# A sandwich layer of banded attention and a feed-forward on eight cores: the halo rows in 16 partitions, the clears behind the layernorm of x, and two thirds of its last step by ScalarE

## The chip, the cores and the metric

The kernel runs on the 8 cores of one Trainium2 chip, in two dies of four. The metric is the device time of the slowest core in microseconds (us). Times inside a profile are counted from the start of that core's span. No data goes from one core to another.

## The reference

x has 8192 rows of 2048 (float32). With `ln` for a layernorm over the 2048 columns, the reference computes

```
x = x + ln(attn(ln(x)))       # attn: 32 heads of 64, each query sees keys i-8 .. i+7,
                              # scores scaled and weighted by distance, softmax, projection, bias
x = x + ln(ffn(ln(x)))        # ffn: 2048 -> 2048 with sign(W) * max|W|, gamma, beta
```

Each core owns 1024 rows and also needs 8 rows ahead of them and 8 behind them as keys and values: the halo.

## The kernel before

Every engine has its own instruction list, written out by hand, and takes it in order; semaphores tie the lists together. The stages are: (1) the front, which makes `lnT`, the layernorm of x, transposed and in bf16, and at the same time begins with (2) the 36 value tiles of 16 matmuls (L504); (3) 64 steps of attention with the query and key projections between them (L528); (4) the projection and the feed-forward in eight row tiles each (L591), with the rest of the layer.

**The front.** It has nine units. Unit 0 is the halo, 16 rows; units 1 to 8 are 128 rows each. One unit u passes through:

1. its load, `x_in[u]`: units 1 to 8 by the GpSimd queue (L399) in the order x1, first half of the value weights, x2, second half, x3 to x8, then the next block of value weights. `xbuf` has five places, so x6, x7 and x8 are issued only when units 1, 2 and 3 have been applied. The halo comes by SyncE's queue (L366, L367), into partitions 0 to 7 and 64 to 71 of a cleared buffer
2. `x_stats(u)` by VectorE: four BN statistics (L784) and their aggregate (L787)
3. `rstd` by ScalarE: Ln and Exp of the variance (L688, L689)
4. the last step of the layernorm by VectorE, (x - mean) * rstd to bf16 (L842), which raises `applied`
5. 16 transposes by TensorE in two halves (L487), each half into a PSUM bank of its own
6. `x_copy(u)`: VectorE copies the first half to `lnT` (L792) and raises `tx_v`; ScalarE copies the second (L660) and raises `tx_s`.

The lists run one unit ahead of their copies. VectorE's order for a unit is `x_stats(u)`, `x_copy(u-1)`, last step of u, and for u = 4, 6, 8 a copy of a value tile (`v_copy`). ScalarE's order is `rstd(u)`, `x_copy(u-1)`, and for u = 5, 7 a `v_copy`. TensorE's order is the transposes of units 0 and 1 and then, for each value tile n: its first 8 matmuls, the transposes of unit n + 2 (while there is one), its last 8 matmuls. The first half of tile n waits until both engines have copied unit n + 1:

```
t.wait_ge(tx_v, min(vt + 1, 8) + 1)
t.wait_ge(tx_s, min(vt + 1, 8) + 1)
```

and a transpose of unit u also waits until the copies of unit u - 1 have emptied its bank. After tile 6 there are no transposes left, and TensorE runs through value tiles alone.

**Clears.** Before unit 0, VectorE clears the halo's buffer (L826), `KTz`, `pstrip` and the last block of `VTOK` (L829 to L831), and makes `rolled`, a rotated identity (L833, L834). The halo's load waits for the first of these. `KTz`, `pstrip` and `rolled` are first used by attention, the cleared block of `VTOK` by value tile 8.

**SyncE's queue** loads the masks, the projection's bias and the first two feed-forward strips when all nine units are applied.

Of the kernel before, what the change touches and what calls it, by code (L numbers as in the profile page):

```python
# [15 lines left out]
D = 2048  # L16
# [18 lines left out]
LAG_T = LAG_S + 3  # L35
QUERIES = 2 * KWIN
LEAD = 3
FFN0 = 1 + NT - LEAD
# [19 lines left out]
def build_program():  # L58
# [15 lines left out]
    def sem(name):  # L74
        return nc.alloc_semaphore(name)
# [3 lines left out]
    at_small = base  # L79
    at_attn = at_small + 2592  # L80
    at_lnp = at_attn + 32 * OWN
# [7 lines left out]
    def place(name, cols, dtype, at, rows=128):  # L89
        return nc.alloc_sbuf_tensor_at(name, [rows, cols], dtype, offset=at)  # L90
# [14 lines left out]
    vwbf = place("vwbf", 2 * FULLW, BF16, at_attn)  # L105
    projb = place("projb", D, F32, at_lnp)
    fin = place("fin", 16, F32, at_small + 2528)
# [4 lines left out]
    xhalo = place("xhalo", D, F32, at_f + 56704)  # L112
    lnbf = place("lnbf", 2 * D, BF16, at_wp + 24576)
# [37 lines left out]
    ident_in_sem = sem("ident_in")  # L151
    halo_zero = sem("halo_zero")
    consts = sem("consts")
    var_ready = sem("x_var_ready")
    padded = sem("padded")
    x_in = [sem(f"x_in{u}") for u in range(9)]
    rstd_ready = sem("x_rstd_ready")
    applied = sem("x_applied")
    half_tx = sem("x_half_transposed")
# [7 lines left out]
    def xs(u):  # L167

        slot = (u - 1) % 5
        if u == 0:  # L170
            return xhalo[:]
        return xbuf[:, slot * D:(slot + 1) * D] if slot < 3 else (xbuf3 if slot == 3 else xbuf4)[:]

    def ls(u):
        return lnbf[:, u % 2 * D:(u % 2 + 1) * D]

    def mvc(u, i, n=1):
        return mv[:, 4 * u + i:4 * u + i + n]

    def x_evac(u, half):  # L180
        src = tpx[half].rearrange("p (k c) -> p k c", c=128)
        parts = [(0, 0, 8), (64, 8 + OWN, 8)] if u == 0 else [(0, 8 + 128 * (u - 1), 128)]
        return [(lnT3[:, half * 8:(half + 1) * 8, do:do + wd], src[:, :, so:so + wd]) for so, do, wd in parts]
# [176 lines left out]
    with nc.Block() as blk:  # L360

        @blk.sync
        def _(q):
            q.dma_start(out=ident[:], in_=ident_in).then_inc(ident_in_sem, 16)
            q.wait_ge(halo_zero, 1)
            q.dma_start(out=xhalo[0:8, :], in_=x_hbm[0:8, :]).then_inc(x_in[0], 16)  # L366
            q.dma_start(out=xhalo[64:72, :], in_=x_hbm[OWN + HALO:OWN + 2 * HALO, :]).then_inc(x_in[0], 16)  # L367
            q.wait_ge(applied, 9)
            q.dma_start(out=maskm[:], in_=masks[0]).then_inc(mask_in[0], 16)
# [25 lines left out]
        def _(g_):  # L395
            def load_x(u):
                if u >= 6:
                    g_.wait_ge(applied, u - 4)
                g_.dma_start(out=xs(u), in_=x_hbm[HALO + 128 * (u - 1):HALO + 128 * u, :]).then_inc(x_in[u], 16)  # L399
# [23 lines left out]
            load_v(1, 0, HALFW, FULLW)  # L423
            for u in range(3, 9):
                load_x(u)
# [53 lines left out]
        def _(t):  # L479
            def x_transposes(u):  # L480
                t.wait_ge(applied, u + 1)
                for half in range(2):
                    if u:
                        t.wait_ge(tx_v if half == 0 else tx_s, u)
                    for k8 in range(8):
                        kc = half * 8 + k8
                        last = t.transpose(tpx[half][:, k8 * 128:(k8 + 1) * 128],  # L487
                                           ls(u)[:, kc * 128:(kc + 1) * 128], ident[:])
                    last.then_inc(half_tx, 1)
# [114 lines left out]

            t.wait_ge(padded, 4)
            for G in range(STEPS + LAG_T):
# [49 lines left out]
        def _(s):  # L656
# [6 lines left out]
            def v_copy(n):  # L663
                if n == 17:
                    s.wait_ge(padded, 4)
# [25 lines left out]
            s.wait_ge(consts, 2)  # L691
# [84 lines left out]
        def _(v):  # L776
# [3 lines left out]
            def x_stats(u):  # L780

                v.wait_ge(x_in[u], 32 if u == 0 else 16)
                for c in range(4):
                    done = v_own.on(v.bn_stats(bnst[:, 24 * u + 6 * c:24 * u + 6 * c + 6],  # L784
                                               xs(u)[:, c * NB:(c + 1) * NB]))
                v.wait_ge(v_own.sem, done)
                v.bn_aggr(mvc(u, 0, 2), bnst[:, 24 * u:24 * u + 24]).then_inc(var_ready, 1)  # L787

# [6 lines left out]
            def v_copy(n):  # L795
                if n == 8:
                    v.wait_ge(padded, 4)
# [34 lines left out]
            v.wait_ge(ident_in_sem, 16)  # L832
            v.tensor_copy(rolled[:, 0:16], ident[:, 112:128])  # L833
            v.tensor_copy(rolled[:, 16:128], ident[:, 0:112]).then_inc(padded, 1)  # L834
            for u in range(9):
                x_stats(u)
                if u:
                    x_copy(u - 1)
                if u >= 2:
                    v.wait_ge(half_tx, 2 * (u - 2) + 2)  # L840
                v.wait_ge(rstd_ready, u + 1)
                v.tensor_scalar(ls(u), xs(u), mvc(u, 0), mvc(u, 2), ALU.subtract, ALU.mult).then_inc(applied, 1)  # L842
# [6 lines left out]
            v.wait_ge(padded, 4)  # L849
            v.wait_ge(mask_in[0], 16)  # L850
# [214 lines left out]
```

## Time and profile before

| what | before |
|---|---|
| median of 3 runs | 728.91 us (727.24 to 729.54) |
| the profiled execution's own time | 729.89 us |
| its span on the slowest core (core 3) | 728.4 us |
| spans of all cores | 720.7 to 728.4 us |
| TensorE busy | 659.3 us, 91% |
| VectorE busy | 425.7 us, 58% |
| ScalarE busy | 331.3 us, 45% |
| GpSimd busy | 205.5 us, 28% |
| data moved by DMA | 98.66 MB, mean 135 GB/s |

Between the span and the profiled time lie 1.49 us of start and end. In rows of instructions the first number is the start, the second the time from the first start to the last end of a merged group; in square brackets stands how long the engine had been idle and what ended that. PE is TensorE, PEld its weight loads, DVE VectorE, ACT ScalarE, POOL GpSimd, SPq SyncE's queue. In rows of DMA issues the last number is the time from issue to landing. Idle time of an engine that nothing waits for costs nothing.

### The profile page before, as it was taken

What the parts mean: (1) busy time and instruction counts of PE and PEld (TensorE: products, weight loads), DVE (VectorE), ACT (ScalarE), POOL (GpSimd) and SP (SyncE); (2) the same over time, 40 slices, a digit from 0 to 9 for tenths busy, and PEclk for the clock granted to TensorE, in tenths of its full rate; (3) what the DMA queues carried; (4) which work ended last, traced back from release to release, by engine and by line L of the source; (5) the groups of instructions that cost most, each with busy time, mean ns of one, the idle gap of its engine ahead of it and who ended that gap; (6) DMA issues with size and microseconds to landing.
All of it is one profiled execution on the core that took longest, in us unless ns stands there. A gap on an engine that the chain in (4) does not pass through costs nothing.

```text
span 728.4 us, 13295 instructions; the slowest of 8 cores (720.7 to 728.4 us)
## 1 busy us (share of the span) xinstructions
PE 659.3 (91%) x4048; PEld 356.1 (49%) x4048; DVE 425.7 (58%) x798; ACT 331.3 (45%) x888; POOL 205.5 (28%) x271
## 2 busy tenths in 40 slices
PE   0599999999999999999999999999989958689993
PEld 0354444445666666666666665444434424334441
DVE  7894110112667777777777776324776648777655
ACT  0222000001577777777777778402433404544244
POOL 2000010000666666666666667200001000000000
PEclk9999999999999999999999999999999989989997
DMA  8995949930447767667667765953434393744453
GB/s 187 278 233 142 177 71 154 169 53 1 59 62 118 125 119 122 121 117 123 117 117 119 120 112 91 162 154 61 143 115 139 104 334 117 231 146 144 145 199 118
DMA packets 18101, 98.66 MB, mean 135 GB/s; under 512 B 2274, under 2 KB 2274, under 8 KB 11490
## 3 DMA queue, kind: packets, MB, share of 16 engines
q0 software_dynamic: 10656, 67.11, 44.2%
q1 hardware_dynamic: 7378, 30.71, 17.2%
q8 instruction: 36, 0.59, 0.3%
q14 instruction: 31, 0.25, 0.1%
HBM read 114.59 MB, written 16.78 MB: 180 GB/s over the span
## 4 chain that ended last, share of the span: by engine, by line
PE 67%; DVE 11%; issue 10%; DMA 6%; ACT 3%; POOL 1%; DVEq 1%; ACTq 0%; POOLq 0%
PE bank L528 30%; PE bank L504 15%; PE bank L591 13%; DMA y_scratch<-abuf 6%; DVE bnst L784 3%; DVE abuf L921 3%; PE bank L544 2%; PE bank L552 2%; PE bank L553 2%; PE bank L565 2%; DVE abuf L961 1%; ACT tstrip L718 1%; ACT xnb L773 1%; DVE KTz L829 0%; DVE pstrip L830 0%
## 5 line engine op out<-in xcount | busy, mean ns | idle before, releaser
L528 PE MATMUL bank<-lnT,wbf 128*128 128x512 bf16 (+2 forms) x1280 | 248.4, 338 | 0.0
L528 PEld LDWEIGHTS bank<-lnT,wbf 128*128 128x128 bf16 x1280 | 122.8, 98 | 83.8 <-issue 0.4
L417 POOL TENSOR_TENSOR tstrip<-tstrip,maskb 128x288 f32<-128x288 f32 x128 | 93.5, 731 | 158.4 <-DVE tstrip L807 158.4
L504 PE MATMUL bank<-vwbf,lnT 128*128 128x512 bf16 (+1 forms) x576 | 128.8, 382 | 5.2 <-ACT lnT L660 5.2
L718 ACT ACTIVATE tstrip<-tstrip,soft 128x144 f32<-128x144 f32 x256 | 103.6, 405 | 44.4 <-DVE soft L866 44.0
L591 PE MATMUL bank<-Wp,attnT 128*128 128x512 bf16 x512 | 115.0, 383 | 0.5 <-DVE attnT L861 0.5
L591 PE MATMUL bank<-Wf,attnT 128*128 128x512 fp8e4 x512 | 113.7, 384 | 0.0
L807 DVE TENSOR_TENSOR tstrip<-bank,maskm 128x288 f32<-128x288 f32 x128 | 58.1, 454 | 64.1 <-PE bank L544 63.9
L504 PEld LDWEIGHTS bank<-vwbf,lnT 128*128 128x128 bf16 (+1 forms) x576 | 54.8, 97 | 75.4 <-issue 12.4
L591 PEld LDWEIGHTS bank<-Wf,attnT 128*128 128x128 bf16 x512 | 50.6, 99 | 61.2 <-issue 3.1
L591 PEld LDWEIGHTS bank<-Wp,attnT 128*128 128x128 bf16 x512 | 50.1, 99 | 59.3 <-issue 3.2
L453 POOL TENSOR_TENSOR pstrip<-tstrip,soft 128x576 bf16<-128x576 f32 x64 | 73.8, 1153 | 15.1 <-DVE soft L855 14.0
L800 DVE CAST VTOK<-bank 128x512 bf16<-128x512 f32 (+1 forms) x18 | 12.4, 689 | 89.1 <-PE bank L504 89.1
L668 ACT CAST VTOK<-bank 128x512 bf16<-128x512 f32 (+1 forms) x18 | 10.6, 586 | 92.9 <-PE bank L504 92.9
L708 ACT COPY ptbuf<-bank 128x576 bf16<-128x576 bf16 x64 | 41.0, 640 | 21.5 <-PE bank L553 20.8
L467 POOL DMA_DIRECT2D y_scratch<-abuf x8 | 4.4, 547 | 162.4 <-DVE abuf L961 162.4
L718 ACT ACTIVATION_READ_ACCUMULATOR tstrip<-tstrip,soft 128x1 f32 x256 | 48.1, 188 | 0.0
L866 DVE TENSOR_REDUCE soft<-tstrip 128x4 f32<-128x576 f32 x64 | 47.4, 740 | 0.0
L823 DVE TENSOR_REDUCE amaxc<-fwstage 128x1 f32<-128x1024 f32 x32 | 38.5, 1210 | 5.2 <-DMA fwstage<-ffn_wt 5.2
L683 ACT ACTIVATE Wf<-fwstage 128x1024 fp8e4<-128x1024 f32 x32 | 33.2, 1042 | 11.4 <-DMA fwstage<-ffn_wt 11.4
L552 PE MATMUL bank<-identb,pstrip 128*128 128x128 bf16 x256 | 35.3, 218 | 2.0 <-POOL pstrip L453 2.0
L544 PE MATMUL bank<-KTz,QT 128*128 128x288 bf16 x128 | 36.6, 286 | 0.0
(95 smaller groups left out, 696.3 us busy)
## 6 DMA issues: line engine op xcount, KB each, us to landing
fwstage<-ffn_wt SPq DMA_DIRECT2D x32, 512.0 KB, 6.6
wbf<-qk_strips POOLq DMA_DIRECT2D x32, 512.0 KB, 6.3
xbuf<-x_shard POOLq DMA_DIRECT2D x8, 1024.0 KB, 14.8
Wp<-proj_wt POOLq DMA_DIRECT2D x4, 2048.0 KB, 33.7
xre<-x_shard POOLq DMA_DIRECT2D x8, 1024.0 KB, 8.7
y_scratch<-abuf POOLq DMA_DIRECT2D x8, 1024.0 KB, 6.3
ybuf<-y_scratch SPq DMA_DIRECT2D x8, 1024.0 KB, 6.8
out<-fbuf POOLq DMA_DIRECT2D x7, 1024.0 KB, 8.6
```

The costliest lines, as they stand in the source:

```text
L417: g_.tensor_add(ts(g)[:, i * QUERIES:(i + 1) * QUERIES], ts(g)[:, i * QUERIES:(i + 1) * QUERIES], maskb[:, b * QUERIES:(b + 1) * QUERIES]) ...
L453: g_.tensor_mul(pu(r_)[:, :, 0:KWIN], ts3(r_), rtotal(r_)[:, :, None].broadcast_to([128, 4, KWIN])).then_inc(normed, 1)
L504: last = t.matmul(vbanks[n % 4][0:rows, :], lnT[:, kc * TOK + 128 * vt:kc * TOK + 128 * vt + rows], vwbf[:, (ng % 2) * FULLW + kc * NB:(ng ...
L528: last = t.matmul(qkbanks[gg % 3][:, 0:wd], wslot(2 * ph + is_k)[:, kc * 128:(kc + 1) * 128], lnT[:, kc * TOK + c0:kc * TOK + c0 + wd], st ...
L544: t.matmul(sbanks[i][:, 0:QUERIES], qt(ph)[:, 128 * b:128 * b + 128], ktz(ph)[:, :, 128 * b:128 * b + KWIN], start=True, stop=True).then_i ...
L552: t.transpose(tbank[:, u * 256:u * 256 + 128], pu(g)[:, u, 0:128], ident[:])
L591: last = t.matmul(bank(i), attnT[:, kc * OWN + 128 * t_:kc * OWN + 128 * t_ + 128], rhs, start=(kc == 0), stop=(kc == 15))
L708: s.copy(pt(h), tbank.rearrange("p (u c) -> p u c", c=256)[:, :, 0:KWIN]).then_inc(p_ev, 1)
L718: last = s.activation(ts3(m)[:, u, :], ts3(m)[:, u, :], AF.Exp, bias=neg_max(m)[:, u:u + 1], accum_out=total(m)[:, u:u + 1])
L807: v.tensor_mul(ts(g)[:, i * QUERIES:(i + 1) * QUERIES], sbanks[i][:, 0:QUERIES], maskm[:, b * QUERIES:(b + 1) * QUERIES]).then_inc(masked, 1)
L823: v.reduce_max(amaxc[:, i:i + 1], fw_slot(i), axis=AX.X, apply_absolute_value=True).then_inc(amaxed, 1)
L866: v.reduce_max(neg_max(m), ts3(m), axis=AX.X, negate=True).then_inc(maxed, 1)
```

## The change

Five things change, all in the front.

- **Halo.** The 16 halo rows lie in partitions 0 to 15 of `xhalo`, which has 16 partitions and isn't cleared. Their two loads are the first in SyncE's queue, ahead of the identity. All steps of unit 0 work on 16 partitions (`x_rows(0)`), and the transposes give 16 columns.
- **Clears.** `KTz` is cleared by VectorE after its last `x_copy(8)`, and `rolled` and `pstrip` after `v_copy(6)`. The block of `VTOK` is cleared by GpSimd between the issues of x5 and x6, with a semaphore of its own, `v_padded`.
- **Last step.** For the units 0, 2, 3, 5, 6 and 8 (`ACT_APPLIES`) ScalarE does the last step. VectorE negates the mean (one more instruction with 1 element per partition), ScalarE makes rstd, then -mean * rstd, then one Identity activation of 2048 elements with scale and bias. Units 1, 4 and 7 stay as they were.
- **Semaphores.** `applied` becomes `applied_v` and `applied_s`; `x_applied(u)` gives the one and its count for unit u. Who waited for `applied` now waits for the unit that matters.
- **A first Exp.** ScalarE runs an Exp of one element (`warm`) ahead of its loop.

```
@@ sync
-            q.wait_ge(halo_zero, 1)
+            q.dma_start(out=xhalo[0:8, :], in_=x_hbm[0:8, :]).then_inc(x_in[0], 16)
+            q.dma_start(out=xhalo[8:16, :], in_=x_hbm[OWN + HALO:OWN + 2 * HALO, :]).then_inc(x_in[0], 16)
             q.dma_start(out=ident[:], in_=ident_in).then_inc(ident_in_sem, 16)
-            q.wait_ge(applied, 9)
+            q.wait_ge(*x_applied(7))
+            q.wait_ge(*x_applied(8))
@@ gpsimd
-                    g_.wait_ge(applied, u - 4)
+                    g_.wait_ge(*x_applied(u - 5))
...
+            g_.memset(VTOK4[:, :, 8, :], 0.0).then_inc(v_padded, 1)
@@ scalar
+            def x_apply(u):
+                rows = x_rows(u)
+                s.wait_ge(s_own.sem, s_own.on(s.activation(mvc(u, 2)[0:rows], mvc(u, 1)[0:rows], AF.Ln,
+                                                          bias=epsv[0:rows, :])))
+                s.wait_ge(s_own.sem, s_own.on(s.activation(mvc(u, 2)[0:rows], mvc(u, 2)[0:rows], AF.Exp, scale=-0.5)))
+                s.wait_ge(s_own.sem, s_own.on(s.activation(mvc(u, 3)[0:rows], mvc(u, 0)[0:rows], AF.Identity,
+                                                          scale=mvc(u, 2)[0:rows])))
+                if u >= 2:
+                    s.wait_ge(half_tx, 2 * (u - 2) + 2)
+                s.activation(ls(u)[0:rows, :], xs(u), AF.Identity, scale=mvc(u, 2)[0:rows],
+                             bias=mvc(u, 3)[0:rows]).then_inc(applied_s, 1)
+            s.wait_ge(consts, 3)
+            s.activation(warm[:], warm[:], AF.Exp)
             for u in range(9):
-                rstd(mvc(u, 2), mvc(u, 1), u + 1, var_ready, epsv).then_inc(rstd_ready, 1)
+                if u in ACT_APPLIES:
+                    s.wait_ge(var_ready, u + 1)
+                    x_apply(u)
+                else:
+                    rstd(mvc(u, 2), mvc(u, 1), u + 1, var_ready, epsv).then_inc(rstd_ready, 1)
                 if u:
                     x_copy(u - 1)
@@ vector, x_stats
+                then(v.bn_aggr(mvc(u, 0, 2)[0:rows], bnst[0:rows, 24 * u:24 * u + 24]))
+                v.tensor_scalar(mvc(u, 0)[0:rows], mvc(u, 0)[0:rows], -1.0, None, ALU.mult).then_inc(var_ready, 1)
@@ vector, main list
-            v.memset(xs(0), 0.0).then_inc(halo_zero, 1)
-            v.memset(KTz[:], 0.0).then_inc(padded, 1)
-            v.memset(pstrip[:], 0.0).then_inc(padded, 1)
-            v.memset(VTOK4[:, :, 8, :], 0.0).then_inc(padded, 1)
...
             x_copy(8)
-            for n in range(6, 36, 2):
+            v.memset(KTz[:], 0.0).then_inc(padded, 1)
+            v_copy(6)
...
+            v.memset(pstrip[:], 0.0).then_inc(padded, 1)
+            for n in range(8, 36, 2):
                 v_copy(n)
```

## Rows read from the trace of the kernel before

**Rows 1.** The chain that ended last: its longest piece (start us, us, what).

```profile
64.20 102.58 PE bank L504 x472
```

**Rows 2.** Timeline of the start: clears, statistics of unit 0, table load.

```profile
4.16 3.52 DVE L829 MEMSET KTz<- 128x4160 bf16 x1 [0.81 <-issue]
12.33 1.76 DVE L831 MEMSET VTOK<- 128x2048 bf16 x1 [0.38 <-issue]
14.12 2.47 DVE L784 BATCH_NORM_STATS2 bnst<-xhalo 128x6 f32<-128x512 f32 x4
17.03 1.28 ACT L688 ACT_TABLE_LOAD   x1 [17.03 <-DVE mv L787]
```

**Rows 3.** DMA issues of x2, and of x3: KB, us from issue to landing.

```profile
xbuf<-x_shard POOLq DMA_DIRECT2D x1, 1024.0 KB, 16.8
...
xbuf<-x_shard POOLq DMA_DIRECT2D x1, 1024.0 KB, 25.9
```

**Rows 4.** Timeline of the GpSimd queue: issues of x2, and of x3 to x5.

```profile
2.79 0.54 POOL L399 DMA_DIRECT2D xbuf<-x_shard  x1
...
3.82 1.60 POOL L399 DMA_DIRECT2D xbuf<-x_shard  x3
```

**Rows 5.** A stretch of 3 us: busy times, granted clock, share of the DMA engines, GB/s.

```profile
27.00:30.00 3.00, 0.64 (x5) 0.26 (x4) 2.65 (x5) 1.40 (x3) 0.00 (x0) 1.00 1.02 322
```

**Rows 6.** Timeline of tile 0 and of units 2 and 3, with their neighbours.

```profile
29.75 3.57 PE L504 MATMUL bank<-vwbf,lnT 128*128 128x512 bf16 x8 [2.36 <-ACT lnT L660]
30.07 2.47 DVE L784 BATCH_NORM_STATS2 bnst<-xbuf 128x6 f32<-128x512 f32 x4
...
34.14 0.69 DVE L792 COPY lnT<-bank 128x1024 bf16<-128x1024 bf16 x1 [1.24 <-PE bank L487]
...
34.75 1.34 DVE L842 TENSOR_SCALAR lnbf<-xbuf,mv 128x2048 bf16<-128x2048 f32 x1
36.00 2.46 DVE L784 BATCH_NORM_STATS2 bnst<-xbuf 128x6 f32<-128x512 f32 x4
```

**Rows 7.** Timeline of a later unit: statistics, rstd, copy, half a tile, transposes.

```profile
41.48 2.47 DVE L784 BATCH_NORM_STATS2 bnst<-xbuf 128x6 f32<-128x512 f32 x4
...
42.28 1.06 PE L487 MATMUL bank<-identb,lnbf 128*128 128x128 bf16 x16
...
44.41 0.30 ACT L688 ACTIVATE mv<-mv,epsv 128x1 f32<-128x1 f32 x1 [3.99 <-DVE mv L787]
44.80 0.20 ACT L689 ACTIVATE mv<-mv 128x1 f32<-128x1 f32 x1
44.91 0.99 ACT L660 COPY lnT<-bank 128x1024 bf16<-128x1024 bf16 x1
...
46.05 1.89 PE L504 MATMUL bank<-vwbf,lnT 128*128 128x512 bf16 x8 [0.98 <-ACT lnT L660]
...
47.77 1.06 PE L487 MATMUL bank<-identb,lnbf 128*128 128x128 bf16 x16
```

**Rows 8.** Timeline: the last unit's transposes and copy, and a later tile's copy.

```profile
63.14 1.06 PE L487 MATMUL bank<-identb,lnbf 128*128 128x128 bf16 x16
63.86 0.69 DVE L792 COPY lnT<-bank 128x1024 bf16<-128x1024 bf16 x1 [1.54 <-PE bank L487]
...
80.05 0.69 DVE L800 CAST VTOK<-bank 128x512 bf16<-128x512 f32 x1 [6.33 <-PE bank L504]
```

**Rows 9.** Groups of ScalarE's instructions by shape: count, busy us, mean ns, idle.

```profile
L773 ACT ACTIVATE xnb<-abuf 128x2048 bf16<-128x2048 f32 x8 | 15.3, 1912 | 14.0 <-DVE abuf L961 14.0
...
L750 ACT ACTIVATE fbuf<-fbuf,tst 128x2048 f32<-128x2048 f32 x7 | 14.7, 2097 | 7.8 <-DVE tst L966 7.8
```

**Rows 10.** Timeline of TensorE behind two idle times of the last stage.

```profile
541.27 1.05 PE L651 MATMUL bank<-identb,xnb 128*128 128x128 bf16 x16 [3.39 <-DVE xnb L925]
...
656.76 1.05 PE L651 MATMUL bank<-identb,xnb 128*128 128x128 bf16 x16 [3.20 <-DVE xnb L925]
```

**Rows 11.** The stretch behind the first of them, columns as in rows 5.

```profile
542.20:545.60 3.40, 3.40 (x12) 1.27 (x10) 3.20 (x6) 1.42 (x4) 0.00 (x0) 0.52 0.00 0
```

More of the change, by code:

```diff
@@ L36 @@
 QUERIES = 2 * KWIN
+ACT_APPLIES = (0, 2, 3, 5, 6, 8)
 LEAD = 3
@@ L79, in build_program @@
     at_small = base
-    at_attn = at_small + 2592
+    at_attn = at_small + 2624
     at_lnp = at_attn + 32 * OWN
@@ L111, in build_program @@
     xbuf4 = place("xbuf4", D, F32, at_f + 41088)
-    xhalo = place("xhalo", D, F32, at_f + 56704)
+    xhalo = place("xhalo", D, F32, at_f + 56704, rows=2 * HALO)
     lnbf = place("lnbf", 2 * D, BF16, at_wp + 24576)
@@ L155, in build_program @@
     padded = sem("padded")
+    v_padded = sem("v_padded")
     x_in = [sem(f"x_in{u}") for u in range(9)]
     rstd_ready = sem("x_rstd_ready")
-    applied = sem("x_applied")
+    applied_v = sem("x_applied_v")
+    applied_s = sem("x_applied_s")
     half_tx = sem("x_half_transposed")
@@ L172, in xs, with x_rows, x_applied @@
         return xbuf[:, slot * D:(slot + 1) * D] if slot < 3 else (xbuf3 if slot == 3 else xbuf4)[:]
+    def x_rows(u):
+        return 2 * HALO if u == 0 else 128
+    def x_applied(u):
+        count = len([i for i in range(u + 1) if (i in ACT_APPLIES) == (u in ACT_APPLIES)])
+        return (applied_s if u in ACT_APPLIES else applied_v), count
     def ls(u):
@@ L423, in _ @@
             load_v(1, 0, HALFW, FULLW)
-            for u in range(3, 9):
+            for u in range(3, 6):
+                load_x(u)
+            g_.memset(VTOK4[:, :, 8, :], 0.0).then_inc(v_padded, 1)
+            for u in range(6, 9):
                 load_x(u)
@@ L480, in x_transposes @@
             def x_transposes(u):
-                t.wait_ge(applied, u + 1)
+                t.wait_ge(*x_applied(u))
+                rows = x_rows(u)
                 for half in range(2):
@@ L486, in x_transposes @@
                         kc = half * 8 + k8
-                        last = t.transpose(tpx[half][:, k8 * 128:(k8 + 1) * 128],
-                                           ls(u)[:, kc * 128:(kc + 1) * 128], ident[:])
+                        last = t.transpose(tpx[half][:, k8 * 128:k8 * 128 + rows],
+                                           ls(u)[0:rows, kc * 128:(kc + 1) * 128], ident[0:rows, 0:rows])
                     last.then_inc(half_tx, 1)
@@ L603, in _ @@
                 v_tile(n, 8, 16)
-            t.wait_ge(padded, 4)
+            t.wait_ge(padded, 3)
             for G in range(STEPS + LAG_T):
@@ L780, in x_stats @@
             def x_stats(u):
+                rows = x_rows(u)
                 v.wait_ge(x_in[u], 32 if u == 0 else 16)
                 for c in range(4):
-                    done = v_own.on(v.bn_stats(bnst[:, 24 * u + 6 * c:24 * u + 6 * c + 6],
+                    done = v_own.on(v.bn_stats(bnst[0:rows, 24 * u + 6 * c:24 * u + 6 * c + 6],
                                                xs(u)[:, c * NB:(c + 1) * NB]))
                 v.wait_ge(v_own.sem, done)
-                v.bn_aggr(mvc(u, 0, 2), bnst[:, 24 * u:24 * u + 24]).then_inc(var_ready, 1)
+                if u not in ACT_APPLIES:
+                    v.bn_aggr(mvc(u, 0, 2)[0:rows], bnst[0:rows, 24 * u:24 * u + 24]).then_inc(var_ready, 1)
+                    return
+                then(v.bn_aggr(mvc(u, 0, 2)[0:rows], bnst[0:rows, 24 * u:24 * u + 24]))
+                v.tensor_scalar(mvc(u, 0)[0:rows], mvc(u, 0)[0:rows], -1.0, None, ALU.mult).then_inc(var_ready, 1)
             def x_copy(u):
@@ L796, in v_copy @@
                 if n == 8:
[L797 removed]
+                    v.wait_ge(v_padded, 1)
                 v.wait_ge(tile_mm, n + 1)
@@ L824, in amax @@
                              apply_absolute_value=True).then_inc(amaxed, 1)
-            v.memset(xs(0), 0.0).then_inc(halo_zero, 1)
             v.memset(epsv[:], EPS).then_inc(consts, 1)
             v.memset(eps2[:], EPS * EPS).then_inc(consts, 1)
-            v.memset(KTz[:], 0.0).then_inc(padded, 1)
-            v.memset(pstrip[:], 0.0).then_inc(padded, 1)
-            v.memset(VTOK4[:, :, 8, :], 0.0).then_inc(padded, 1)
-            v.wait_ge(ident_in_sem, 16)
-            v.tensor_copy(rolled[:, 0:16], ident[:, 112:128])
-            v.tensor_copy(rolled[:, 16:128], ident[:, 0:112]).then_inc(padded, 1)
+            v.memset(warm[:], 0.0).then_inc(consts, 1)
             for u in range(9):
@@ L838, in _ @@
                     x_copy(u - 1)
[L839 to L842, printed above, removed]
+                if u not in ACT_APPLIES:
+                    if u >= 2:
+                        v.wait_ge(half_tx, 2 * (u - 2) + 2)
+                    v.wait_ge(rstd_ready, len([i for i in range(u + 1) if i not in ACT_APPLIES]))
+                    v.tensor_scalar(ls(u), xs(u), mvc(u, 0), mvc(u, 2), ALU.subtract, ALU.mult).then_inc(applied_v, 1)
                 if u in (4, 6, 8):
@@ L845, in _ @@
             x_copy(8)
-            for n in range(6, 36, 2):
+            v.memset(KTz[:], 0.0).then_inc(padded, 1)
+            v_copy(6)
+            v.wait_ge(ident_in_sem, 16)
+            v.tensor_copy(rolled[:, 0:16], ident[:, 112:128])
+            v.tensor_copy(rolled[:, 16:128], ident[:, 0:112]).then_inc(padded, 1)
+            v.memset(pstrip[:], 0.0).then_inc(padded, 1)
+            for n in range(8, 36, 2):
                 v_copy(n)
-            v.wait_ge(padded, 4)
+            v.wait_ge(padded, 3)
             v.wait_ge(mask_in[0], 16)
```

10 lines of the change are left out of this document (4 added, 6 removed).

## The prediction

> **What bounds the kernel now.** I read the chain that ended last first, then the timeline of the first 66 us, then DMA issues with landings, then ScalarE's groups and TensorE's idle times. TensorE sets the end: the longest piece of the chain is 472 value matmuls without a gap from 64.20 us on [rows 1]. They begin right behind the transposes of unit 8, which start at 63.14 [rows 8]. Behind this point TensorE's list is the same before and after the change, and everything later is tied to it. So the whole question is when the transposes of unit 8 start. A microsecond there is a microsecond of the end.
>
> What sets those 63.14 us? The clears keep VectorE until unit 0 starts at 14.12 [rows 2]. From there it has no gap worth the name: statistics, copy and last step follow each other at about 5.2 us a unit (30.07, 36.00, 41.48 [rows 6, 7]). But a second thing has nearly caught up. The load of x3 is issued at 3.82 and lands 25.9 us later, at 29.7 [rows 3, 4]; VectorE takes it up at 30.07 [rows 6]. The DMA engines are full in that stretch, share 1.02 [rows 5], and x3 stands behind x1, x2 and two blocks of value weights in one queue. A start of the statistics 9 us earlier therefore meets data that isn't there.
>
> **The steps and their prices.** I lay out the chain of the new lists, with each link from the nearest row.
>
> - Statistics to the start of ScalarE's last step, 4.15 us: statistics to Ln 2.93 (41.48 to 44.41); 0.25 for the negation of one element and its wait, an estimate after ScalarE's one-element instruction, 0.20 plus a wait of 0.09 (rounded down, as VectorE's are shorter); then Ln to a dependent instruction 0.39 (44.41 to 44.80), and Exp and the new one-element Identity 0.29 each (0.20 and the same wait of 0.09), together 0.97 [rows 7].
> - The last step on ScalarE, 1.95 us until its next instruction. Rows for 2048 elements give 1.91 with bf16 out and 2.10 with float32 out, scale and bias [rows 9]. I take 1.95, bounds 1.86 and 2.05, since the next instruction starts a little before the end. VectorE needs 1.25 for the same (34.75 to 36.00 [rows 6]).
> - ScalarE's copy to the matmuls that wait for it 1.15 (44.91 to 46.05); eight matmuls to the transposes behind them 1.72 (46.05 to 47.77) [rows 7], at the low clock 3.4 (tile 0's row of 3.57 with its end, against 1.89 [rows 6, 7]); transposes to VectorE's copy 0.7 (63.14 to 63.86 [rows 8]); this copy to VectorE's next instruction 0.6 (34.14 to 34.75 [rows 6]).
> - A `v_copy` on VectorE, 0.65, a little under its row of 0.69 [rows 8].
>
> **What goes off the path.** The halo's clear, the three others and `rolled` leave the front. They cost nothing later: VectorE idles 6.33 us between two copies of value tiles [rows 8], and `KTz` with 3.52 us [rows 2] and `pstrip`, nearly as large, each fit into such a gap; the bank of tile 6 is wanted again only four tiles later. Without that cover 7 us would be on the path. GpSimd's clear of `VTOK` takes between VectorE's 1.76 us [rows 2] and, as an estimate, twice that; behind it stands the issue of x6, which waits until unit 1 is applied, about 14.5 by the sum below, while the five loads are issued by 5.4 [rows 4]. Hidden, and x6 stands behind others in a full queue anyway. The halo's loads come first and are small; even landing at 12 they'd be ready before x2. SyncE's masks follow unit 8 as before. The 1.28 us of table load [rows 2] moves into idle time; a second one, if the first Exp loaded a table without Ln, would still lie ahead of x2.
>
> Two things of ScalarE decide the sum. One is whether a copy whose data is ready can pass an instruction that still waits. It can't in the trace: the transposes of unit 4 are over at 43.34, and ScalarE's copy of them starts at 44.91, right behind the Ln and Exp of unit 5, which had waited for VectorE until 44.41 [rows 7]. The Trainium skill says the same (TensorE: Matmul & The Clock Gate, Architectural detail): ScalarE and VectorE take their instructions strictly in order. By that rule the sum below stands at 66.9; if a copy could pass, the same links would give 62.7, and the change would cost nothing.
>
> The other is the price of 2048 elements. The rows give 1.91 and 2.10 [rows 9]. The skill's page on ScalarE (ScalarE: Activation LUTs, Step-by-step) has one element in 0.83 ns whatever the function, an estimate of 1.71 us here; the sum would be 0.9 lower by it. The rows are longer, and I go by them.
>
> **The sum.** The important thing is the order. ScalarE does the last step of unit u ahead of its copy of unit u - 1. The first half of value tile u - 2 waits for this copy, the transposes of unit u stand behind that half tile in TensorE's list, and VectorE's copy of unit u waits for these. Before, only a short rstd stood ahead of the copy. Now a statistics-to-copy delay of 6.1 us (4.15 + 1.95) does, and VectorE, in order, waits in turn. Tile 0's first half begins at 26.85 (x2 lands at 2.79 + 16.8 = 19.6 [rows 3, 4]; + 4.15 + 1.95 + 1.15). Cold matmuls and 16 transposes later its second half ends at about 33 us, and TensorE idles for 4 us. Then, at full clock:
>
> 1. x3 lands 29.7; ScalarE applies unit 3 at 33.85, copies unit 2 at 35.80; tile 1 at 36.95; transposes of unit 3 at 38.68; VectorE's copy 39.37; its last step of unit 4 at 39.97
> 2. + 1.25 + 0.65 of `v_copy`: statistics of unit 5 at 41.9. Before they began at 41.48 [rows 7]. The whole head start is gone here
> 3. unit 5: apply 46.0, copy of unit 4 at 48.0, tile 3 at 49.1, transposes 50.9, VectorE's copy 51.55, then `v_copy`: statistics of unit 7 at 52.8
> 4. unit 6 meanwhile: ScalarE, held by unit 5, a copy and a `v_copy`, applies it at 50.55, copies unit 5 at 52.5; tile 4 at 53.65; transposes 55.4; VectorE's copy 56.1, last step of unit 7 at 56.7; statistics of unit 8 at 57.95
> 5. unit 8: apply 62.1, copy of unit 7 at 64.05, tile 6 at 65.2, its transposes at 66.9.
>
> That is 66.9 against 63.14: 3.8 us later. The same links put through the old order give 62.9 for the old kernel, so the arithmetic is good to some 0.3 us. The data of units 4 to 8 isn't what holds it: each is wanted no more than 3 us earlier than it was, and never waited for, and unit 4's last step waits until 40 for TensorE.
>
> One term more, the clock. TensorE's idle time of 3.39 us in the last stage was followed by a stretch of 3.40 us with a granted clock of 0.52, the 1.2 GHz level [rows 10, 11], worth 1.7 us; behind 3.20 us of idle it stayed at 2.4 GHz [rows 10]. The new list has idle times of about 4.0 us (ahead of tile 1), 3.5 (tile 3) and 2.8 (tile 6). At the first a loss is likely, and tile 1 lies on the chain, so + 1.7: transposes of unit 8 at 68.6, 5.5 us later. A second such stretch at tile 3 gives 70.1, 7.0 later.
>
> The profiled 729.89 is its span of 728.4 and 1.49 around it; with 5.5 more it becomes 735.4. It stands 0.98 above the median, so I predict 728.91 + 5.5 = 734.4 us.
>
> **The rivals.** A measurement here tells about 0.3%, 2.2 us, from no change.
>
> - *Chain as above, one low-clock stretch at tile 1*: 734.4, chance 0.37. Its own range, with ScalarE's step between its bounds (two or three times 0.1 us) and landings 1 us earlier: 733.2 to 735.2.
> - *Clock never falls*: 728.91 + 3.8 = 732.7, chance 0.25. For it: 3.20 us of idle left the clock up. Against: 3.39 didn't.
> - *Clock falls twice or more*: 735.9, up to 738 with a third at tile 6, chance 0.18.
> - *Not slower: x3 lands earlier.* Place: the first link. If the halo's bytes out of the way and different crowding on the shared memory bring x3 down by 2 us or more, to 27.7, and the clock holds, the transposes of unit 8 start by 64.9, + 1.8: 730.7, inside 0.3%. Beyond 2 us VectorE's own pace takes over; with all data at hand the chain still gives 61.5, a gain of 1.6, 727.3. For it: DMA times vary. Against: the engines are full [rows 5] with the same bytes in the same order. Chance 0.14.
> - *Faster by over 0.3%*: needs unit 8's transposes by 60.9, under what the chain gives with all data at hand; a link would have to be much cheaper than its row. Chance 0.06.
> - *The removed clears don't count at all*, that is, nothing but DMA decides: the chain of links 2 to 5 would then not lengthen, and the time be the old one. It falls with link 2 above, and is part of the 0.14.
>
> **The numbers.** Slower 0.80, same 0.14, faster 0.06. The range reaches from the rival with earlier data, 730.5, to between the second and third loss of clock, 737.5; below it lies some 0.08, above it some 0.05.
>
> **What the new profile would show.** Statistics of unit 0 at about 5, of unit 3 at 29.7 with a wait for the DMA of `xbuf`; a gap of TensorE of about 4 us ahead of tile 1; VectorE's copies (L792's successor) waiting for TensorE in units 3, 5 and 6, where they never waited for long; ScalarE's copy behind each 1.9 us activation; transposes of unit 8 at 67 to 70. I'm wrong if they start before 63; most likely by data that came earlier, or by an order of copies other than I read.

## The result, and the profile after

The change makes the kernel slower: 736.1 us (median of 5 runs) against 728.91, a ratio of 1.0083 with a 95% interval of 1.0046 to 1.0120. Forecast were 734.4 us, in a range of 730.5 to 737.5. Some executions of a kernel here fall into a slower state of the chip, such as one of these five at 786.13 us; the ratios and their intervals leave them out, the medians given here don't, and the four others lie at 731.97 to 737.53 us with a median of 734.8. The same kernel timed a second time, on another occasion, gave 1.0043 (0.9998 to 1.0087). That interval reaches 1.0, so by the times alone the loss is small and its size is open. In that second comparison, as in the experiments 1 to 4, the kernel before was itself spread over 727 to 738 us; for that reason the steps below are judged by marks inside the traces and the times are given beside them. The profiled execution was the fastest of the five, 731.97 us, its slowest core being core 2 with a span of 730.4 us.

The timeline of core 2 in the changed kernel, cut to the chain that the prediction laid out (start us, us, what; in brackets the idle time ahead and what ended it):

```profile
4.66 2.46 DVE L817 BATCH_NORM_STATS2 bnst<-xhalo 16x6 f32<-16x512 f32 x4 [3.40 <-DMA xhalo<-x_shard]
...
28.56 2.47 DVE L817 BATCH_NORM_STATS2 bnst<-xbuf 128x6 f32<-128x512 f32 x4 [5.58 <-DMA xbuf<-x_shard]
...
30.03 1.06 PE L502 MATMUL bank<-identb,lnbf 128*128 128x128 bf16 x16
...
31.75 0.29 ACT L708 ACTIVATE mv<-mv,epsv 128x1 f32<-128x1 f32 x1 [5.20 <-DVE mv L824]
...
32.87 2.09 ACT L715 ACTIVATE lnbf<-xbuf,mv 128x2048 bf16<-128x2048 f32 x1
34.87 0.99 ACT L675 COPY lnT<-bank 128x1024 bf16<-128x1024 bf16 x1
...
36.01 2.82 PE L519 MATMUL bank<-vwbf,lnT 128*128 128x512 bf16 x8 [3.20 <-ACT lnT L675]
...
38.62 1.82 PE L502 MATMUL bank<-identb,lnbf 128*128 128x128 bf16 x16
...
39.79 0.69 DVE L829 COPY lnT<-bank 128x1024 bf16<-128x1024 bf16 x1 [4.34 <-PE bank L502]
...
42.25 2.46 DVE L817 BATCH_NORM_STATS2 bnst<-xbuf 128x6 f32<-128x512 f32 x4
...
49.69 2.85 PE L519 MATMUL bank<-vwbf,lnT 128*128 128x512 bf16 x8 [3.17 <-ACT lnT L675]
...
54.71 2.46 DVE L817 BATCH_NORM_STATS2 bnst<-xbuf 128x6 f32<-128x512 f32 x4
...
60.00 2.46 DVE L817 BATCH_NORM_STATS2 bnst<-xbuf 128x6 f32<-128x512 f32 x4
...
67.55 3.55 PE L519 MATMUL bank<-vwbf,lnT 128*128 128x512 bf16 x8 [3.00 <-ACT lnT L675]
...
70.92 1.07 PE L502 MATMUL bank<-identb,lnbf 128*128 128x128 bf16 x16
```

Read it from the top. The halo is there at 4.66, where VectorE used to be clearing until 14.12 [rows 2]. But VectorE then waits for data three times, the last for 5.58 us, and takes up x3 at 28.56, only 1.5 us before the old 30.07 [rows 6]. The transposes of unit 2 start at 30.03 and are over at 31.1, so their copy could start then. But ScalarE's list has the last step of unit 3 first, which runs from 32.87, and only behind it, at 34.87, comes the copy of unit 2, on which tile 1 waits until 36.01. The transposes of unit 3 stand behind this half tile, VectorE's copy waits 4.34 us for them, and the statistics of unit 5 begin at 42.25, later than the 41.48 of before [rows 7]. The same pattern returns at tile 3 and at tile 6. The transposes of unit 8 start at 70.92, in [rows 8] at 63.14.

The chain that ended last, between 25 and 72 us, goes through the same instructions (start us, us, what). What it calls "issue" at 32.91 is the last step on ScalarE: the chain has given it no name, but L715 fills just that time above.

```profile
3.83 24.64 DMA xbuf<-x_shard
28.56 2.48 DVE bnst L817 x4
...
32.91 1.96 issue
34.87 1.00 ACT lnT L675
35.87 0.14 issue
36.01 2.82 PE bank L519 x8
38.83 0.87 PE bank L502 x8
```

The waits of TensorE from 15 to 170 us (us in total, times, longest) say the same in one line; of the four, one is the start of tile 0, and the others stand ahead of tiles 1, 3 and 6.

```profile
PE bank L519 <- ACT lnT L675: 19.5, 4, 10.2
```

Behind each of these three idle times core 2 lost the clock, as the granted clock of three stretches shows (the column behind POOL; 1.00 is the 2.4 GHz level and 0.50 the 1.2 GHz level, and values between them are stretches with both; the others as in rows 5):

```profile
36.00:40.00 4.00, 3.99 (x21) 2.37 (x22) 0.21 (x1) 0.26 (x2) 0.58 (x2) 0.60 0.97 326
49.69:53.10 3.41, 3.41 (x16) 1.75 (x17) 0.00 (x0) 3.08 (x5) 0.00 (x0) 0.61 0.96 166
67.50:71.00 3.50, 3.45 (x10) 1.28 (x11) 0.00 (x0) 0.00 (x0) 0.00 (x0) 0.51 0.60 186
```

Core 6 of the same execution had idle times of 1.34, 3.49 and 3.00 us ahead of the same tiles, and kept 2.4 GHz through all three. Its timeline:

```profile
47.45 1.89 PE L519 MATMUL bank<-vwbf,lnT 128*128 128x512 bf16 x8 [3.49 <-ACT lnT L675]
...
63.91 1.89 PE L519 MATMUL bank<-vwbf,lnT 128*128 128x512 bf16 x8 [3.00 <-ACT lnT L675]
65.63 1.06 PE L502 MATMUL bank<-identb,lnbf 128*128 128x128 bf16 x16
```

**One mark for all kernels.** The first matmul of the attention (L528 before, L543 with the change) is reached by TensorE with nothing but a fixed list behind the last transposes, so it measures the front. It is taken per core from the group of that line, and the mean over the eight cores is given. From there to the last matmul of the same line it is the same time in both kernels, 279.8 us on every core to within 0.1.

| kernel | first attention matmul, mean | median of all runs, us | ratio to before | 95% interval |
|---|---|---|---|---|
| before | 166.7 | 728.91 | | |
| the change | 172.4 | 736.1 | 1.0083 | 1.0046 to 1.0120 |
| the change, again | 172.4 | 736.44 | 1.0043 | 0.9998 to 1.0087 |
| split alone | 174.0 | 738.11 | 1.0052 | 1.0012 to 1.0092 |
| clock kept | 171.0 | 731.6 | 0.9971 | 0.9932 to 1.0009 |
| x3 earlier | 170.0 | 731.83 | 1.0024 | 0.9989 to 1.0060 |
| transposes first | 164.9 | 726.55 | 0.9954 | 0.9922 to 0.9986 |
| copy first | 164.2 | 726.11 | 0.9896 | 0.9824 to 0.9969 |
| halo and clears | 164.2 | 727.46 | 0.9895 | 0.9821 to 0.9969 |
| VectorE alone, x3 and transposes first | 162.9 | 725.43 | 0.9944 | 0.9916 to 0.9972 |
| split, x3 and transposes first | 163.0 | 725.22 | 0.9937 | 0.9901 to 0.9974 |
| the same, clock kept | 161.3 | 724.39 | 0.9897 | 0.9815 to 0.9979 |

Each ratio is to runs of the kernel before made together with it: a median of 735.02 us for the experiments 1 to 4, 728.81 for 5 to 8, 730.02 for 9 and 10. So a ratio of one of these sets can't be held against one of another: 0.9896 for the copy first and 0.9944 for VectorE alone don't make the first the faster kernel. The experiments 9 and 10 ran on another chip than 1 to 8; the change's mark is 172.4 on both occasions.

The change is 5.7 us late at the mark. Its eight cores stood 2.1 to 8.3 us behind their own times of before there, since each lost the clock zero to three times.

### The profile page after: what moved, and what is told of

The parts are those of the page before. It is cut to its first block, busy times and chain, and to the rows that moved or that the text cites. A ratio compares the mean times of both kernels' runs of the same rounds, so it can differ in the third digit from the quotient of the medians.

```text
span 730.4 us, 13263 instructions; the slowest of 8 cores (723.4 to 730.4 us)
## 1 busy us (share of the span) xinstructions
PE 659.6 (90%) x3991; PEld 357.5 (49%) x4048; DVE 415.6 (57%) x797; ACT 344.8 (47%) x901; POOL 207.3 (28%) x272
## 4 chain that ended last, share of the span: by engine, by line
PE 67%; issue 10%; DVE 9%; DMA 9%; ACT 3%; POOL 1%; DVEq 0%; ACTq 0%; POOLq 0%
PE bank L543 30%; PE bank L519 15%; PE bank L606 14%; DMA y_scratch<-abuf 5%; DMA xbuf<-x_shard 3%; DVE abuf L959 3%; PE bank L559 2%; PE bank L567 2%; PE bank L568 2%; PE bank L580 2%; DVE bnst L817 1%; ACT tstrip L750 1%; DVE abuf L999 1%; ACT xnb L805 1%; ACT lnT L675 0%
## 5 line engine op out<-in xcount | busy, mean ns | idle before, releaser
L543 PE MATMUL bank<-lnT,wbf 128*128 128x347 bf16 (+2 forms) x1249 | 244.2, 337 | 1.6
L543 PEld LDWEIGHTS bank<-lnT,wbf 128*128 128x128 bf16 x1280 | 122.8, 98 | 83.8 <-issue 0.4
L519 PE MATMUL bank<-vwbf,lnT 128*128 128x512 bf16 (+1 forms) x563 | 130.6, 390 | 20.2 <-ACT lnT L675 19.5
L606 PE MATMUL bank<-Wf,attnT 128*128 128x512 fp8e4 x512 | 116.0, 390 | 0.0
L606 PE MATMUL bank<-Wp,attnT 128*128 128x512 bf16 x499 | 111.9, 379 | 1.2 <-DVE attnT L899 0.5
```

Source lines behind the costliest of these rows:

```text
L519: last = t.matmul(vbanks[n % 4][0:rows, :], lnT[:, kc * TOK + 128 * vt:kc * TOK + 128 * vt + rows], vwbf[:, (ng % 2) * FULLW + kc * NB:(ng ...
L543: last = t.matmul(qkbanks[gg % 3][:, 0:wd], wslot(2 * ph + is_k)[:, kc * 128:(kc + 1) * 128], lnT[:, kc * TOK + c0:kc * TOK + c0 + wd], st ...
L606: last = t.matmul(bank(i), attnT[:, kc * OWN + 128 * t_:kc * OWN + 128 * t_ + 128], rhs, start=(kc == 0), stop=(kc == 15))
```

## The experiments

**1. ScalarE's copy first.** The split, the halo and the clears stay; in the units that ScalarE applies, only two instructions change places.

```
                 for u in range(9):
+                if u in ACT_APPLIES and u:
+                    x_copy(u - 1)
                 if u in ACT_APPLIES:
                     s.wait_ge(var_ready, u + 1)
                     x_apply(u)
...
-                if u:
+                if u and u not in ACT_APPLIES:
                     x_copy(u - 1)
```

> The changed kernel, but in the units that ScalarE applies its copy of the unit before stands ahead of the last step. Theory (the order of ScalarE's list costs the time): the same links give the transposes of unit 8 at about 63.6 us, 0.5 behind the kernel before instead of 7.8, TensorE's waits ahead of tiles 1, 3 and 6 fall from 3 us to under 2, and the time comes to 729.4 us, within 0.3% of before. Rival (ScalarE's 2.1 us in place of VectorE's 1.35 us, wherever it stands): at least six times 0.75 us stay, transposes of unit 8 at 67 or later, 733 us. Rival (late data): nothing moves, 735 us.

Measured: transposes of unit 8 at 60.7 as a mean over the cores (68.8 with the change, 63.1 before). The waits of TensorE, 15 to 170 us, on this kernel's slowest core:

```profile
PE bank L519 <- DVE lnT L831: 10.2, 2, 7.2
PE bank L502 <- ACT lnbf L715: 3.1, 3, 1.1
```

No wait for ScalarE's copy is left. TensorE now waits for the last step itself, 1.1 us at the longest. Both rivals fall: ScalarE still takes 2.1 us six times, and the data lands when it did. The order of two instructions turns a loss of 5.7 us at the mark into a gain of 2.5. The result is 3 us better than I expected. Half of that fits x3, which VectorE takes up near 28.3 on these cores and not at 29.7; the other half I haven't traced.

**2. Halo and clears alone.** `ACT_APPLIES = (0,)`.

> The changed kernel with ScalarE applying unit 0 alone: halo and clears as changed, the last step of units 1 to 8 by VectorE. Theory: the start is early, x3 still lands at 28 to 30, so nearly all of the 9 us saved by the clears is lost in waiting for x2 and x3; VectorE's pace from there gives the transposes of unit 8 at 61.8, 1.3 before the old kernel, 727.6 us. Rival (the clears were worth their 9 us and the split took all of it away): unit 8 at 54, 720 us.

Measured: transposes of unit 8 at 60.7, attention at 164.2. The timeline shows VectorE waiting, then pacing:

```profile
19.71 2.47 DVE L817 BATCH_NORM_STATS2 bnst<-xbuf 128x6 f32<-128x512 f32 x4 [4.66 <-DMA xbuf<-x_shard]
...
29.03 2.47 DVE L817 BATCH_NORM_STATS2 bnst<-xbuf 128x6 f32<-128x512 f32 x4 [4.35 <-DMA xbuf<-x_shard]
...
55.17 2.46 DVE L817 BATCH_NORM_STATS2 bnst<-xbuf 128x6 f32<-128x512 f32 x4
```

An early start of 9 us is worth 2.5 us at the mark; late data eats the rest. This part of the change is good, and the split took 8.2 us from it. It also shows that with the copy first the split gained nothing over VectorE alone: both reach 164.2.

**3. The split alone.** `x_rows(0)` is 128 and the halo lies in partitions 0 and 64 of its cleared buffer again; all clears and `rolled` stand ahead of unit 0.

```
+            v.memset(xs(0), 0.0).then_inc(halo_zero, 1)
...
+            v.memset(KTz[:], 0.0).then_inc(padded, 1)
+            v.memset(pstrip[:], 0.0).then_inc(padded, 1)
+            v.memset(VTOK4[:, :, 8, :], 0.0).then_inc(v_padded, 1)
```

> Halo, its clear and the other clears as in the kernel before (VectorE reaches unit 0 at about 14), the split of the last step as changed. Theory: from x3 on the chain is that of the changed kernel, so unit 8's transposes start at 67.8 with the clock kept and 69 to 71 with it lost, 733 to 735 us, the same as with the whole change. Rival (the split shortens VectorE's list by 0.8 us a unit, and early start and split only hurt together): 63 or earlier, 729 us or less.

Measured: transposes of unit 8 at 70.2, attention at 174.0, 7.2 late. The split does its harm without any of the rest. With it the early start is worth no more than 1.6 us.

**4. The clock kept.**

```
+                if k0 == 0 and n in (1, 3, 6):
+                    for kc in range(6):
+                        t.matmul(banks[6][:, :], lnT[:, kc * TOK + 8:kc * TOK + 136],
+                                 vwbf[:, kc * NB:(kc + 1) * NB], start=(kc == 0), stop=(kc == 5))
```

> The changed kernel with six extra matmuls of 512 columns into an unused bank ahead of the waits of tiles 1, 3 and 6, 1.3 us inside idle times of 1.3 to 3.5 us. Theory (a third of the loss is the low clock behind these idle times): no first half of a tile takes over 1.9 us any more, unit 8's transposes start at 65.5 to 67.8 over the cores, some 2 to 3 us earlier than in the changed kernel, 732.5 us. Rival (clock has no part in it, or the extra matmuls just take TensorE's time): 735 us or more.

Measured: transposes of unit 8 at 67.4 as a mean, 65.4 to 68.8; attention at 171.0, 1.4 us earlier than with the change. Half of what I expected. Counting first halves of tiles 1, 3 and 6 that took over 1.9 us on the eight cores, there are six, against 15 with the change, and none is left ahead of tile 6. Core 0 is one of the six:

```profile
48.70 2.88 PE L523 MATMUL bank<-vwbf,lnT 128*128 128x512 bf16 x8 [2.20 <-ACT lnT L679]
...
66.56 1.89 PE L523 MATMUL bank<-vwbf,lnT 128*128 128x512 bf16 x8 [1.70 <-ACT lnT L679]
```

So the extra matmuls helped and were too few: nine of the fifteen losses went, and 1.4 us with them. How large the clock's whole part is, the cores tell better. With the change, cores 6, 3 and 5 took up x3 within 0.25 us of each other (27.65 to 27.89). Core 6 lost the clock at no tile and reached the mark at 169.2; cores 3 and 5 lost it at two and were there at 172.4 and 172.2. That is 1.5 to 1.6 us a loss. Of the mean delay of 5.7 us some 3.2 are then the clock (172.4 against 169.2 on the core without a loss) and 2.5 the waits themselves, an estimate from one core; the three cores of this experiment that kept the clock at these tiles (2, 4 and 6) stand at 169.0 to 170.3, 2.3 to 3.6 behind before. The two can't be told apart as causes, though: the clock falls behind the idle times that the waits make.

**5. Transposes ahead of the tile.** ScalarE's list is that of the change; the edit is on TensorE.

```
             for n in range(36):
-                v_tile(n, 0, 8)
                 if n + 2 <= 8:
                     x_transposes(n + 2)
+                v_tile(n, 0, 8)
                 v_tile(n, 8, 16)
```

> The changed kernel, ScalarE's list untouched, but TensorE's list has the transposes of unit n + 2 ahead of the whole of tile n instead of between its halves. Theory (the loss comes from the pair: half a tile that waits for ScalarE's late copy, and transposes standing behind it): either side of the pair can be undone. Transposes no longer stand behind the waiting half tile, the waits of about 3 us ahead of tiles 1, 3 and 6 go, and the first matmul of the attention starts at 164.6 us as a mean over the cores, against 166.7 before, 172.4 with the change, 164.2 with the copy first; 727 us. Rival (ScalarE's list alone is at fault: its copies are as late as before): 170 or later, 733 us.

Measured: attention at 164.9, expected 164.6. The slowest core's timeline at units 3 and 4:

```profile
33.55 2.09 ACT L715 ACTIVATE lnbf<-xbuf,mv 128x2048 bf16<-128x2048 f32 x1
35.55 0.99 ACT L675 COPY lnT<-bank 128x1024 bf16<-128x1024 bf16 x1
35.89 0.61 PE L502 MATMUL bank<-identb,lnbf 128*128 128x128 bf16 x8 [2.37 <-ACT lnbf L715]
...
37.13 3.62 PE L519 MATMUL bank<-vwbf,lnT 128*128 128x512 bf16 x16
```

The copy still comes behind the last step. But the transposes start 0.34 us after the copy does: they no longer stand behind a half tile that waits for the copy. The fault lies in the pair of lists, and either one can be mended. The rival, that ScalarE's list alone is to blame, falls.

**6. x3 earlier.**

```
             load_x(2)
+            load_x(3)
             load_v(1, 0, HALFW, FULLW)
-            for u in range(3, 6):
+            for u in range(4, 6):
                 load_x(u)
```

> The changed kernel with the load of x3 ahead of the second half of the first value weights, so that it lands at about 22 instead of 28.5. Theory: the late data takes only the head start; with x3 six us earlier the chain of ScalarE's and TensorE's lists still paces the units, the statistics of unit 4 now wait for x4 instead, and the first matmul of the attention comes 1 us earlier, 171.5, 735 us. Rival (late data causes the loss): statistics of all later units move by 5 us and more, 167 or earlier, 729 us.

Measured: attention at 170.0, 2.5 us earlier than with the change, between the two theories. The timeline:

```profile
23.21 2.46 DVE L818 BATCH_NORM_STATS2 bnst<-xbuf 128x6 f32<-128x512 f32 x4
...
31.51 0.69 DVE L830 COPY lnT<-bank 128x1024 bf16<-128x1024 bf16 x1 [5.21 <-PE bank L503]
...
32.35 2.47 DVE L818 BATCH_NORM_STATS2 bnst<-xbuf 128x6 f32<-128x512 f32 x4
...
36.03 3.62 PE L520 MATMUL bank<-vwbf,lnT 128*128 128x512 bf16 x16
...
45.76 3.57 PE L520 MATMUL bank<-vwbf,lnT 128*128 128x512 bf16 x8 [3.49 <-ACT lnT L676]
```

Unit 3's statistics come at 23.21, five us earlier. Unit 4's come only at 32.35, and hardly for want of their data, as my theory had it: VectorE stood for 5.21 us ahead of its copy of unit 2, whose transposes stand behind the first half of tile 0, and the statistics follow that copy. On the eight cores this wait is 4.5 to 5.2 us, and a wait for x4 behind it 1.0 us at the most. It is the pair of lists again, one unit earlier. The idle time ahead of tile 1 is gone, with its loss of clock, which I hadn't counted; those ahead of tiles 3 and 6 are as with the change. Late data is a cause of the lost head start. It isn't the cause of the loss: with x3 early the mark is still 3.2 us behind the kernel before.

**7 and 8. Both lists mended and the data earlier, with and without the split.** Edits 5 and 6, once with `ACT_APPLIES = (0, 3, 4, 5, 6)` and once with `(0,)`.

> Transposes ahead of the tile, x3 ahead of the second weights, and ScalarE applies units 0, 3, 4, 5 and 6 (units 7 and 8, the last of the chain, by VectorE, whose step is shorter). Theory: VectorE has about 4.4 us a unit and TensorE 4.5, so TensorE runs through nearly without a wait from unit 2 on; first matmul of the attention at 160.7 us, 723 us. Rival (the split gains nothing over VectorE alone): the same as the next kernel, 162.

> As the kernel before it in this call, but ScalarE applies unit 0 alone. Theory: VectorE paces the units at 5.2 us, TensorE waits 0.5 to 1.2 us at some of them; first matmul of the attention at 161.9 us, 1.2 behind the split one, 724 us. Rival (load and TensorE's order gain nothing without the split): 164.2 as with halo and clears alone, 727 us.

Measured: 163.0 with the split, 162.9 without. I had expected 160.7 and 161.9. The split again gained nothing, and this time the trace of its eight cores says why. Core 3, the slowest:

```profile
38.54 1.86 PE L503 MATMUL bank<-identb,lnbf 128*128 128x128 bf16 x16 [2.96 <-ACT lnbf L716]
40.20 5.72 PE L520 MATMUL bank<-vwbf,lnT 128*128 128x512 bf16 x16
```

and core 4 of the same execution:

```profile
38.18 0.61 PE L503 MATMUL bank<-identb,lnbf 128*128 128x128 bf16 x8 [1.88 <-ACT lnbf L716]
38.97 0.61 PE L503 MATMUL bank<-identb,lnbf 128*128 128x128 bf16 x8 [0.18 <-ACT lnT L676]
39.41 3.62 PE L520 MATMUL bank<-vwbf,lnT 128*128 128x512 bf16 x16
```

Unit 4's data lands at about 32, TensorE idles for 3 us ahead of its transposes, and runs the next 16 matmuls in 5.72 instead of 3.62 us. On core 4, with 1.88 us of idle, nothing of the kind, and its attention begins at 161.3. Seven of the eight cores lost the clock there with the split, and two (1 and 6) with VectorE alone; the six others of that kernel stand at 162.4 to 163.4, 162.9 as a mean.

**9. The same with extra matmuls in that idle time.**

```
+                if n == 2:
+                    for kc in range(8):
+                        t.matmul(banks[6][:, :], lnT[:, kc * TOK + 8:kc * TOK + 136],
+                                 vwbf[:, kc * NB:(kc + 1) * NB], start=(kc == 0), stop=(kc == 7))
```

> The kernel with all three edits and eight extra matmuls of 512 columns (1.7 us) in TensorE's idle time of about 3 us ahead of the transposes of unit 4, where seven of its eight cores then showed the low clock and the eighth, with 1.9 us of idle, didn't. Theory (only that stretch kept the split from gaining): the first matmul of the attention moves from 163.0 to 161.3 us, where the eighth core had it, 723.5 us. Rival (extra matmuls push the transposes back, or the clock falls elsewhere): 163 or later, 725 us.

Measured: 161.3 as a mean over all eight cores, as expected. Core 3:

```profile
36.54 1.89 PE L618 MATMUL bank<-vwbf,lnT 128*128 128x512 bf16 x8
39.51 0.61 PE L503 MATMUL bank<-identb,lnbf 128*128 128x128 bf16 x8 [1.08 <-ACT lnbf L720]
40.30 0.61 PE L503 MATMUL bank<-identb,lnbf 128*128 128x128 bf16 x8 [0.18 <-ACT lnT L680]
40.74 3.62 PE L520 MATMUL bank<-vwbf,lnT 128*128 128x512 bf16 x16
```

This version is the fastest of all at the mark, 5.4 us ahead of the kernel before and 11.1 ahead of the change. It is also 1.6 ahead of the cores of experiment 8 that kept the clock, as core 4 of experiment 7 is. That suggests that with both lists mended and the clock kept the split gains something over VectorE alone after all; it isn't shown, since experiment 9 ran on another chip and VectorE alone with extra matmuls wasn't run. By its time, ratio 0.9897 (0.9815 to 0.9979), it beats the kernel before, and by 1.0043 (0.9998 to 1.0087) in the same set the change too. Its interval and those of the experiments 7 and 8 overlap, so that it beats them is shown at the mark alone.

**10. The change again.**

> The changed kernel itself once more, for the size of its loss. By its first runs and by the first matmul of the attention, 5.7 us later than before as a mean over the cores, 0.5% to 0.9% slower; the cores differ with how often each loses the clock, so 170 to 175 us for that matmul, and no two runs need agree on which core is last.

Measured: mean of the mark 172.4 as the first time, cores from 169.2 to 174.7; cores 1, 2, 3, 4 and 7, which lost the clock twice each, at 173.6 and later, and cores 0, 5 and 6, with none, none and one short loss, at 169.2, 169.8 and 170.2.

## Why the prediction was right, point by point

**What bounds it, and late data: right.** VectorE waited for x3, 4.8 to 6.1 us on the eight cores. x3 was taken up at 27.7 to 29.0, not 29.7, about 1.4 us earlier than on the core I had read. Experiment 2 sizes the data's part: of an early start of 9 us it leaves 2.5.

**The pair of lists: right, and it is the cause.** The links measured on core 2: statistics to ScalarE's last step 4.31 (28.56 to 32.87; forecast 4.15, the difference being mostly the wait ahead of the last step), last step to the next instruction 2.00 (forecast 1.95), copy to tile 1.14 (1.15). The instruction for 2048 elements took 2.09, at the upper end of [rows 9], as that row with scale and bias had said. Undoing either half of the pair removed the loss (experiments 1 and 5), and so did taking the split away (2). With the pair left as it is, the mark stayed behind the kernel before by 7.2, 4.3 and 3.2 us (3, 4, 6). ScalarE's strict order is seen once more: the transposes of unit 2 were over at 31.1, and ScalarE's copy of them started at 34.87, right behind the last step of unit 3. The Trainium skill states this order (TensorE: Matmul & The Clock Gate, Architectural detail), and the trace agrees.

**The price of 2048 elements: right by the rows, the other price misread.** From the 0.83 ns an element of the Trainium skill (ScalarE: Activation LUTs, Step-by-step) the prediction made 1.71 us for the instruction. The Trainium skill states that figure for a filled pipe. For a whole instruction it adds 186 ns, and about 93 ns for each scale or bias that is read by partition (ScalarE: Activation LUTs, What ACT_TABLE_LOAD costs), an estimate of 2.08 us here. The 2.09 measured agrees with it.

**The sum: right in its total, partly by luck.** The prediction added 3.8 us for the chain with the clock kept and 1.7 for one loss of it. On core 6, which lost no clock, the transposes of unit 8 start at 65.6; forecast were 66.9 for x3 at 29.7, so 64.9 for its x3 at 27.7. The chain is 0.7 to 0.8 us longer than its links said. Most of that is in the two links above, 0.16 and 0.05 us too short each time; ScalarE's last step stands on the chain four times (units 3, 5, 6 and 8), and not two or three times as the range of the first rival has it. Against that x3 came 1.4 us earlier than the sum had it, as a mean. And the clock was priced too low: the cores lost it 1.9 times on average and not once, worth some 3 us and not 1.7. These misses cancel. The mean over the cores is 68.8, which is 5.7 behind the mean before, against 5.5. The mechanism is borne out step by step; that the number came so near is luck in part.

**The clock: right in kind, too low in its chance.** I gave 0.37 to one loss and 0.18 to two or more. Per core it was: none once, one twice, two or three five times. The idle time ahead of tile 1 came out shorter than the 4.0 us I had, 1.3 to 3.2; ahead of tile 3 it was 2.9 to 3.5 (3.5), ahead of tile 6 3.0 (2.8). And the metric takes the slowest of eight cores, so what has a small chance on one core is likely on one of them; I hadn't drawn this. The step from 734.4 to 736.1 is no sign of it, since the four runs around it lie at 731.97 to 737.53.

**Hidden edits: right.** `KTz` and `pstrip` were cleared at 73.2 and 78.2 in VectorE's idle time and no tile waited. GpSimd's clear took 1.87 us. The one table load came at 1.34, and there was no second.

**What I hadn't foreseen** is that a part of the delay isn't seen at the end of the profiled execution: 5.7 us late at the mark, its slowest span is only 2.0 longer. On the slowest cores it is 7.8 us late at the mark (174.5 on core 2 against 166.7 on core 3), and 5.8 of them are gone by the end. From the last matmul of the mark's line (L528, now L543) to the end the cores took 277.6 us before and 275.0 after, as means; in the second trace of the change 273.8. The profiled execution was also the fastest of its five: the median of 734.8 us above is 5.9 behind the kernel before. The chain there goes through the round trip of `y_scratch`. In the changed kernel:

```profile
517.61 5.85 DMA y_scratch<-abuf
...
535.30 5.11 DMA y_scratch<-abuf
...
566.93 5.17 DMA y_scratch<-abuf
```

Each of the two chains has six such pieces of over 5 us, and not every one got shorter (one of the changed kernel took 6.51). Their sum is 39.0 us after and 45.3 before, which is the 5.8 us of the slowest cores and a little more. The cores of the changed kernel reach that stage 5.6 us apart instead of 0.6, and might crowd the memory less. Over all twelve traces the longest such ends (277.6 and 278.5 us) belong to kernels whose cores come 0.6 and 1.5 us apart and the shortest (273.8, 273.8 and 275.0) to those with 4.9 to 5.6. But experiment 6, with 5.4 us apart, had 275.5, as had experiment 5 with 1.9, and I made no run that spreads the cores on purpose. Why the pieces are shorter stays open.

**Open as well:** what decides whether a core loses the clock behind an idle time of about 2 to 3.8 us. The runs show both outcomes for 3.00 and for 3.49 us, on cores of one execution. The shortest idle time with a loss behind it in the fronts of these kernels is in experiment 8, core 6: 1.95 us, transposes still at full speed, and then 15 matmuls in 5.01 us instead of 3.40.

```profile
37.81 1.05 PE L503 MATMUL bank<-identb,lnbf 128*128 128x128 bf16 x16 [1.95 <-DVE lnbf L875]
38.99 5.01 PE L520 MATMUL bank<-vwbf,lnT 128*128 128x512 bf16 x15
```

## What to carry to other kernels

When a step moves from one in-order engine to another, price its place in the new engine's list before its duration: what stands behind it there now waits for everything that it waits for, and here 2 us of work a unit on an engine that was idle more than half the time cost 8. Follow the wait in a circle: a copy behind the long step, a tile behind the copy, the next transposes behind the tile, the first engine behind the transposes. Then ask of every microsecond saved at the start which data will be there to use it, and measure a front at a mark of its own, since the end of an eight-core kernel is the slowest of eight cores and blurs it.

## What the runs showed of the hardware

- TensorE at the 1.2 GHz level behind short idle times: a loss behind 2.96 us (experiment 7, core 3, 16 matmuls in 5.72 us), behind 2.20 us (experiment 4, core 0, eight in 2.88) and behind 1.95 us (experiment 8, core 6, 15 in 5.01, granted clock 0.68 in the stretch from 39 to 44 us); none behind 3.49 us (the change, core 6) and behind 3.78 us (experiment 6, core 2, eight in 1.89). I had taken 3.2 us for harmless by one row.
- An Identity activation of 2048 elements, float32 to bf16, with scale and bias by partition takes 2.09 us; the Square of 2048 elements to bf16, with neither, has 1.91 [rows 9]. On 16 partitions it takes the same 2.09 us.
- Sixteen transposes of the halo took 0.57 us on 16 rows, in the same early stretch in which those of unit 1 took 1.87 on 128.
